# The softmax sums' inverses of an attention phase, sent by the sync engine's queue instead of ScalarE's

## The chip, the cores and the metric

The program runs on one core of one Trainium2 chip. The metric is the device time of one execution in microseconds (us), which is the time of that core. The unchanged kernel took 2614.75 us, the median of 3 runs (2609.27 to 2626.25).

## What is computed

A block of three parts over x of shape 16 x 512 x 256 in fp32: half of a feed-forward part, a causal attention, half of the feed-forward part again. The change lies in the attention:

```python
def _L0_attn_ref(x, Wq, bq, Wkv, bkv, Wo, bo):
    H, DQK, DV = (16, 64, 64)
    b, s, e = x.shape
    q = x @ Wq + bq
    kv = x @ Wkv + bkv
    k, v = jnp.split(kv, [H * DQK], axis=-1)
    q = _rope(q.reshape(b, s, H, DQK).transpose(0, 2, 1, 3))
    k = _rope(k.reshape(b, s, H, DQK).transpose(0, 2, 1, 3))
    v = v.reshape(b, s, H, DV).transpose(0, 2, 1, 3)
    scores = jnp.einsum('bhqd,bhkd->bhqk', q, k) * (1.0 / np.sqrt(DQK))
    scores = jnp.where(causal[None, None], scores, -jnp.inf)
    probs = jax.nn.softmax(scores, axis=-1)
    out = jnp.einsum('bhqk,bhkd->bhqd', probs, v)
    return out.transpose(0, 2, 1, 3).reshape(b, s, H * DV) @ Wo + bo

x = x + 0.5 * _L0_ffn_ref(_layernorm(x), ...)
x = x + _L0_attn_ref(_layernorm(x), ...)
x = x + 0.5 * _L0_ffn_ref(_layernorm(x), ...)
```

## The kernel before, in words

The attention phase works on 16 batches, one after the other, and on the 16 heads of a batch in 8 pairs. So it has 128 units (batch, pair). The order on each engine is written out by hand: `program` calls a function `slot` once per step, and in one slot an engine does the parts of several units that are a few steps apart. `Slot.p` is the number of the pair (0 to 7) within the batch, and `t.has(p + 2)` says that a unit so far ahead or behind exists. The waits are semaphore counts; `need_held` waits and then counts on a semaphore of its own.

What one unit goes through, with the names in the profile:

- TensorE projects queries and keys into `att_ps_z` (L1353), two slots ahead. ScalarE moves them to `att_z_sb` with the bias (L1608).
- The rotary turn needs halves of 32 partitions swapped. SP's queue does it with four DMAs, `swap` (L1370, `att_zs<-att_z_sb`, 128 KB each). GpSimd then multiplies and adds (L1426, L1427, L1429), ScalarE takes the high part of the keys and queries (L1614), GpSimd (L1434) and VectorE (L1500) the low parts.
- TensorE makes the scores (L1765). VectorE adds the mask (L1518) and takes the largest value of each row (L1522). ScalarE takes the exponentials with the sums (L1630): for the four tiles of 128 queries in the order 3, 2, 1, 0. Tiles 3 and 2 go to `att_far`, tiles 1 and 0 to `att_prob`.
- The exponentials of tiles 3 and 2 are turned by way of DRAM: `put` on ScalarE's queue writes `att_far` to `last_tiles_blocks` (L1642, one DMA of 896 KB), `get` on SP's queue reads it in another order into `att_got` in the next slot (L1385, four DMAs of 224 KB), and VectorE transposes blocks of 32 x 32 (`turn`, L1534). `att_got` is a single buffer, so a `get` waits for the `turn` before it.
- The exponentials of tiles 1 and 0 are transposed on TensorE (L1803) and copied by ScalarE in two parts, `copy_near` (L1654) and `copy_next` (L1659).
- TensorE mixes the values (L1818, L1823) into `att_ps_p`.
- The inverse of the sums must stand on all the partitions of a head. VectorE makes it and transposes it (`reciprocals`, L1526 and L1529, into `att_rsumT`). `rows` writes it to DRAM (`inverse_sums`, one DMA of 16 KB). `spread` on SP's queue reads it back, repeated over 64 partitions, into `att_R` (L1377, two DMAs of 128 KB). VectorE multiplies the mixed values by it (`divide`, L1540).
- ScalarE and VectorE split the result into a high and a low part (L1664, L1545), TensorE multiplies by Wo (L1353), and VectorE adds it up in `att_acc` (L1494).
- ScalarE copies the next pair's values to `att_v_sb` (`values`, L1648). TensorE's next projection waits for that copy, because both use the same PSUM bank.

The queue of SP does in one slot, in this order: `swap` of the unit two ahead (it waits for both L1608), `get` of the unit before (it waits for its `put` and for the `turn` before it), `spread` of the same unit (it waits until `rows` has landed), and in three of eight slots a load or store of 512 KB: the residual input at p = 7 (L1402), the next input at p = 0 (L1407), the store of the result at p = 3 (L1413).

`rows` stands on ScalarE's queue before the change: after `copy_next` and before the exponentials of tile 2. `att_rsumT` is a single buffer too: VectorE's next transpose into it waits until `rows` has landed.

## Time and profile before

| | |
|---|---|
| median of 3 runs | 2614.75 us |
| lowest, highest | 2609.27, 2626.25 us |
| the profiled execution | 2626.25 us, of it 2623.5 us from the first to the last instruction |
| TensorE, VectorE, ScalarE, GpSimd busy | 87%, 70%, 55%, 55% of the span |
| granted TensorE clock, mean | 0.974 |
| DMA | 561.57 MB, mean 214 GB/s |

A page of the profile lists per engine the busy time, the groups of instructions by line with the idle time before them and what ended it, and the DMA queues. In the names, PE is TensorE, PEld its weight loads, DVE VectorE, ACT ScalarE, POOL GpSimd, SP SyncE; a "q" behind the name is that engine's sequencer, which issues DMAs and waits while the engine itself may still be busy.

### The profile page before, as it was taken

The numbers are of one execution on the slowest core, as the hardware profiler recorded it, in microseconds if no ns is written. First come the engines' busy times: TensorE is split into PE (matmuls) and PEld (weight loads), VectorE is DVE, ScalarE is ACT, GpSimd is POOL, SyncE is SP. The second block draws the span as 40 slices with busy tenths as digits, with TensorE's granted clock in tenths as the row PEclk, the third lists the DMA queues.
The fourth block names the chain that finished last, engine by engine and source line by source line (L and its number), as shares of the span: only waits on it lengthen the run. The fifth ranks groups of instructions, "written<-read, shape, count | busy, mean of one in ns | idle before, by whom it ended". The sixth has DMA issues, their size and how long they took to land. (4 is left out here: it accounts for less than half of the span.)

```text
span 2623.5 us, 55026 instructions
## 1 busy us (share of the span) xinstructions
PE 2293.0 (87%) x17624; PEld 1793.8 (68%) x17624; DVE 1825.7 (70%) x3128; ACT 1447.8 (55%) x3741; POOL 1434.8 (55%) x1268
## 2 busy tenths in 40 slices
PE   7987899788988988998889889889898878986998
PEld 5753677577777777777777777777777765753676
DVE  5741578487777778777777778778778775741476
ACT  2321444466766766776667667666676652321343
POOL 1100444677677777776677777767777741100342
PEclk9999999899999999999999999999999998999999
DMA  7369553578878888888788887887878876369543
GB/s 249 130 258 409 198 174 119 151 206 220 212 203 222 232 223 220 222 226 215 196 226 219 217 219 214 233 218 205 235 206 223 218 210 214 132 256 409 164 155 101
DMA packets 340248, 561.57 MB, mean 214 GB/s; under 512 B 63616, under 2 KB 274176, under 8 KB 338944
## 3 DMA queue, kind: packets, MB, share of 16 engines
q1 hardware_dynamic: 303104, 438.58, 60.5%
q10 hardware_dynamic: 36864, 119.55, 12.3%
q8 instruction: 139, 2.28, 0.4%
q14 instruction: 141, 1.16, 0.2%
HBM read 329.42 MB, written 161.48 MB: 187 GB/s over the span
## 5 line engine op out<-in xcount | busy, mean ns | idle before, releaser
L1426 POOL TENSOR_TENSOR att_z_sb<-att_z_sb,att_cos 128x512 f32<-128x512 f32 x255 | 336.2, 1318 | 387.9 <-DMA att_zs<-att_z_sb 387.8
L1534 DVE STREAM_TRANSPOSE att_farT<-att_got 128x1792 f32<-128x1792 f32 x128 | 261.0, 2039 | 199.4 <-DMA att_got<-last_tiles_blocks 199.0
L1429 POOL TENSOR_TENSOR att_z_sb<-att_z_sb,att_zs 128x512 f32<-128x512 f32 x255 | 339.3, 1331 | 20.0
L1427 POOL TENSOR_TENSOR att_zs<-att_zs,att_sin 128x512 f32<-128x512 f32 x255 | 342.9, 1345 | 0.0
L1823 PE MATMUL att_ps_p<-att_farT,att_v_sb 128*64 128x128 f32 x3584 | 227.8, 280 | 0.0
L1630 ACT ACTIVATE att_far<-att_ps_w,att_nmax 128x512 f32<-128x512 f32 x256 | 174.2, 688 | 78.2 <-DVE att_nmax L1522 68.6
L1823 PEld LDWEIGHTS att_ps_p<-att_farT,att_v_sb 128*64 128x64 f32 x3584 | 210.7, 142 | 0.0
L1353 PE MATMUL att_ps_z<-att_xT_hi,att_wq_hi 128*128 128x512 f32 x256 | 93.7, 447 | 128.5 <-ACT att_v_sb L1648 123.7
L1434 POOL TENSOR_TENSOR att_kT_lo<-att_z_sb,att_kT_hi 128x512 fp32r<-128x512 f32 x128 | 163.6, 1278 | 47.6 <-ACT att_kT_hi L1614 47.6
L1630 ACT ACTIVATE att_far<-att_ps_x,att_nmax 128x384 f32<-128x384 f32 x256 | 146.6, 578 | 41.6 <-issue 30.0
L1522 DVE TENSOR_REDUCE att_nmax<-att_ps_x 128x2 f32<-128x768 f32 (+1 forms) x256 | 164.9, 686 | 4.4
L1055 POOL TENSOR_TENSOR com_b_kblk<-sh_blkmask,sh_kT 128x128 f32<-128x128 f32 x64 | 32.3, 526 | 242.5 <-POOLq L500 195.0
L1522 DVE TENSOR_REDUCE att_nmax<-att_ps_w 128x2 f32<-128x1024 f32 x128 | 156.7, 1224 | 4.4
L180 POOL TENSOR_SCALAR dis_b_veps<-dis_b_mv 128x4 f32<-128x4 f32 x31 | 13.4, 432 | 266.4 <-DVE dis_b_mv L174 266.4
L1803 PE MATMUL att_ps_z<-sh_ident,att_prob 128*128 128x128 f32 x768 | 140.3, 292 | 3.3 <-ACT att_prob L1630 2.6
L457 ACT ACTIVATE dis_b_prob<-dis_ps_s,dis_b_ebias 128x512 f32<-128x512 f32 x64 | 44.6, 697 | 177.8 <-DVE dis_b_ebias L317 177.8
L1353 PEld LDWEIGHTS att_ps_z<-att_xT_hi,att_wq_hi 128*128 128x128 f32 x256 | 39.1, 192 | 151.5 <-ACT att_v_sb L1648 142.7
L1500 DVE TENSOR_TENSOR att_qT_lo<-att_z_sb,att_qT_hi 128x512 fp32r<-128x512 f32 x128 | 137.0, 1070 | 2.0 <-ACT att_qT_hi L1614 2.0
L1765 PE MATMUL att_ps_x<-att_kT_hi,att_qT_hi 64*128 64x256 f32 (+1 forms) x512 | 128.3, 334 | 4.4 <-ACT att_prob L1630 3.5
L1664 ACT CAST att_oT_hi<-att_ps_p 128x512 fp32r<-128x512 f32 x128 | 75.0, 586 | 99.3 <-DMA att_got<-last_tiles_blocks 69.0
L1608 ACT ACTIVATE att_z_sb<-att_ps_z,att_bk 128x512 f32<-128x512 f32 x128 | 88.5, 691 | 69.9 <-PE att_ps_z L1353 69.9
L1141 PEld LDWEIGHTS com_ps_o<-com_b_U,com_b_pT 128*128 128x128 f32 x512 | 97.9, 192 | 42.6 <-issue 27.7
(248 smaller groups left out, 7171.4 us busy)
## 6 DMA issues: line engine op xcount, KB each, us to landing
last_tiles_blocks<-att_far ACTq DMA_DIRECT2D x128, 896.0 KB, 5.3
att_got<-last_tiles_blocks SPq DMA_DIRECT2D x512, 224.0 KB, 4.8
att_zs<-att_z_sb SPq DMA_DIRECT2D x512, 128.0 KB, 3.2
att_R<-inverse_sums SPq DMA_DIRECT2D x256, 128.0 KB, 3.9
ffn_w<-in_e_W SPq DMA_DIRECT2D x30, 1024.0 KB, 9.4
ffn_wg<-in_e_Wg SPq DMA_DIRECT2D x24, 1024.0 KB, 12.8
x_normalised_transposed<-dis_b_xnT SPq DMA_DIRECT2D x32, 512.0 KB, 3.0
ffn_w<-in_e_W SPq DMA_DIRECT2D x32, 512.0 KB, 15.6
```

The costliest lines, as they stand in the source:

```text
L1353: last = nc.tensor.matmul(ps, lhs[a][ch], rhs[b][ch], start=(i == 0), stop=(i == len(terms) - 1))
L1426: nc.gpsimd.tensor_tensor(z[:, m, i, :], z[:, m, i, :], cos[:], ALU.mult)
L1427: nc.gpsimd.tensor_tensor(zs[:, m, i, :], zs[:, m, i, :], sin[:], ALU.mult).then_inc(sin_s[i].sem, 1)
L1429: nc.gpsimd.tensor_tensor(z[:, m, i, :], z[:, m, i, :], zs[:, m, i, :], ALU.add).then_inc(sum_s[i].sem, 1)
L1434: nc.gpsimd.tensor_tensor(lo[:, u % 2, :], z[:, u % 2, 1, :], hi[:, u % 2, :].bitcast(F32), ALU.subtract)\
L1500: nc.vector.tensor_tensor(lo[:, u % 2, :], z[:, u % 2, 0, :], hi[:, u % 2, :].bitcast(F32), ALU.subtract)\
L1522: nc.vector.tensor_reduce(nmax[:, p % 2, qt, :], scores_of(qt), AX.X, ALU.max, negate=True).then_inc(max_s.sem, 1)
L1534: nc.vector.transpose(farT[:].rearrange("p a (t r) -> p t a r", r=QUAD), got[:]).then_inc(turn_s.sem, 1)
L1630: nc.scalar.activation(dst, src, ACT.Exp, bias=nmax[:, p % 2, qt, hh:hh + 1], accum_out=sums[:, p % 2, hh, qt:qt + 1]).then_inc(exp_s.sem, 1)
L1765: return nc.tensor.matmul(ps, q[a][of_head(hh), p % 2, qt * P:(qt + 1) * P], k[b][of_head(hh), p % 2, 0:wide], start=(m == 0), stop=(m == 2))
L1803: last = nc.tensor.transpose(ps_z[1][:, at:at + P], prob[:, p % 2, hh, PLACE[qt]][:, kb * P:(kb + 1) * P], g.ident[:])
L1823: last = nc.tensor.matmul(mix_bank[of_head(hh), qt * P:(qt + 1) * P], values_of(kb, hh), farT[:, hh * NF + at + kb, :], start=(kb == 0), s ...
```

## The change

`rows` moves from ScalarE's queue to SP's. There it stands between `get` and `spread` of the same unit, with the same two waits: for the transposed inverses, and for the landing of the `spread` before it. Nothing else changes.

```diff
@@ block.sync
+            def rows(j, u):
+                need_held(sp, inv_s, j, 2 * u + 2)
+                need_held(sp, spread_s, j, 32 * u)
+                sp.dma_start(r_dram[u % 2], rsumT[:]).then_inc(row_s.sem, 16)
+
...
                 if t.has(p - 1):
                     get(j, p - 1)
+                    rows(j, p - 1)
                     spread(j, p - 1)
@@ block.scalar
-            def rows(j, u):
-                need_held(act, inv_s, j, 2 * u + 2)
-                need_held(act, spread_s, j, 32 * u)
-                act.dma_start(r_dram[u % 2], rsumT[:]).then_inc(row_s.sem, 16)
-
...
                 if t.has(p - 1):
                     copy_next(j, p - 1)
-                    rows(j, p - 1)
                 if t.has(p):
                     exps(j, p, 2)
                     put(j, p)
```

On ScalarE, in the last slots before the loop over batches, the rows from the second copy to the values' copy stand like this before (L59, L1273 and L1622 belong to waits):

```order
L1614 CAST att_qT_hi<-att_z_sb 128x512
L1273 REGISTER_ALU
L1658 REGISTER_ALU
L1659 COPY att_probT<-att_ps_z 128x256
L59 ISA
L1637 DMA inverse_sums<-att_rsumT 128x32
L1622 REGISTER_ALU
L1630 ACTIVATE att_far,att_sums<-att_ps_x,att_nmax 128x3x4x32 x2
```

and now:

```order
L1620 CAST att_qT_hi<-att_z_sb 128x512
L1273 REGISTER_ALU
L1659 REGISTER_ALU
L1660 COPY att_probT<-att_ps_z 128x256
L1628 REGISTER_ALU
L1636 ACTIVATE att_far,att_sums<-att_ps_x,att_nmax 128x3x4x32 x2
```

The DMA and its held waits are gone between the copy and the exponentials of tile 2; the lines below the change have moved by a few numbers.

On SP's queue, two slots of the same part of the program stand like this before:

```order
L1370 DMA att_zs<-att_z_sb 32x1024 x4
L1385 DMA att_got<-last_tiles_blocks 32x4x448 x4
L1377 DMA att_R<-inverse_sums 64x4x128 x2
L1370 DMA att_zs<-att_z_sb 32x1024 x4
L1385 DMA att_got<-last_tiles_blocks 32x4x448 x4
L1377 DMA att_R<-inverse_sums 64x4x128 x2
```

and now:

```order
L1370 DMA att_zs<-att_z_sb 32x1024 x4
L1390 DMA att_got<-last_tiles_blocks 32x4x448 x4
L1375 DMA inverse_sums<-att_rsumT 128x32
L1382 DMA att_R<-inverse_sums 64x4x128 x2
L1370 DMA att_zs<-att_z_sb 32x1024 x4
L1390 DMA att_got<-last_tiles_blocks 32x4x448 x4
L1375 DMA inverse_sums<-att_rsumT 128x32
L1382 DMA att_R<-inverse_sums 64x4x128 x2
```

The 16 KB write now stands behind all four reads of `get` and directly ahead of the `spread` that waits for it.

## Rows read from the trace of the kernel before

**Rows 1.** Attention phase: us, busy PE, PEld, DVE, ACT, POOL, clock, DMA share, GB/s.

```profile
489.00:2167.00 1678.00, 1467.17 (x13040) 1223.59 (x13039) 1295.05 (x1959) 1143.25 (x3155) 1211.72 (x980) 0.98 0.81 217
```

**Rows 2.** Waits in the same window: us in total, times, longest.

```profile
DVE att_farT L1534 <- DMA att_got<-last_tiles_blocks: 199.0, 76, 7.4
...
PE att_ps_z L1353 <- ACT att_v_sb L1648: 118.4, 94, 3.6
```

**Rows 3.** PE's timeline in a slot without a load: second transposes, next projection.

```profile
1489.17 0.44 PE L1803 MATMUL att_ps_z<-sh_ident,att_prob 128*128 128x128 f32 x2
...
1493.42 0.73 PE L1353 MATMUL att_ps_z<-att_xT_hi,att_wq_hi 128*128 128x512 f32 x2 [1.02 <-ACT att_v_sb L1648]
```

**Rows 4.** ACT's timeline in the same slot.

```profile
1489.64 0.37 ACT L1659 COPY att_probT<-att_ps_z 128x256 f32<-128x256 f32 x1 [0.26 <-PE att_ps_z L1803]
1489.86 0.33 ACTq L1637 DMA_DIRECT2D inverse_sums<-att_rsumT  x1
1490.37 0.58 ACT L1630 ACTIVATE att_far<-att_ps_x,att_nmax 128x384 f32<-128x384 f32 x1 [0.35 <-issue]
...
1492.29 0.59 ACT L1664 CAST att_oT_hi<-att_ps_p 128x512 fp32r<-128x512 f32 x1 [0.68 <-DMA att_got<-last_tiles_blocks]
1492.77 0.59 ACT L1648 COPY att_v_sb<-att_ps_z 128x512 f32<-128x512 f32 x1
```

**Rows 5.** DVE's timeline, same slot: the maxima of tiles 2 and 0, and the turn.

```profile
1488.26 1.29 DVE L1522 TENSOR_REDUCE att_nmax<-att_ps_x 128x2 f32<-128x768 f32 x2
...
1494.59 2.03 DVE L1534 STREAM_TRANSPOSE att_farT<-att_got 128x1792 f32<-128x1792 f32 x1
```

**Rows 6.** Groups by line in the attention phase: tile 2's exponentials, idle time before them.

```profile
L1630 ACT ACTIVATE att_far<-att_ps_x,att_nmax 128x384 f32<-128x384 f32 x256 | 146.6, 578 | 41.6 <-issue 30.0 <-DMA att_R<-inverse_sums 6.2 <-DVE att_nmax L1522 2.8
```

**Rows 7.** ACT's timeline in a slot whose issue waited for the last spread.

```profile
1447.73 0.58 ACT L1630 ACTIVATE att_far<-att_ps_x,att_nmax 128x384 f32<-128x384 f32 x1 [1.55 <-DMA att_R<-inverse_sums]
```

**Rows 8.** What SP's queue waited for in the attention phase: us, times, longest.

```profile
SPq L60 <- DMA inverse_sums<-att_rsumT: 588.2, 126, 8.8
SPq L60 <- ACT att_z_sb L1608: 130.0, 109, 6.5
```

**Rows 9.** SP's queue over the slot of rows 3 to 5.

```profile
1487.95 1.89 SPq L1385 DMA_DIRECT2D att_got<-last_tiles_blocks  x4
1494.74 1.39 SPq L1377 DMA_DIRECT2D att_R<-inverse_sums  x2
1497.26 3.52 SPq L1370 DMA_DIRECT2D att_zs<-att_z_sb  x4
```

**Rows 10.** SP's queue behind the load of the next input (L1407).

```profile
1554.68 1.93 SPq L1385 DMA_DIRECT2D att_got<-last_tiles_blocks  x4
1559.08 1.31 SPq L1377 DMA_DIRECT2D att_R<-inverse_sums  x2
1561.81 3.31 SPq L1370 DMA_DIRECT2D att_zs<-att_z_sb  x4
1566.15 1.93 SPq L1385 DMA_DIRECT2D att_got<-last_tiles_blocks  x4
1572.60 1.59 SPq L1377 DMA_DIRECT2D att_R<-inverse_sums  x2
```

**Rows 11.** ACT's queue in the slot of rows 10.

```profile
1554.26 0.33 ACTq L1637 DMA_DIRECT2D inverse_sums<-att_rsumT  x1
```

**Rows 12.** DVE's turns in the slot of rows 10 and in the next.

```profile
1562.69 2.04 DVE L1534 STREAM_TRANSPOSE att_farT<-att_got 128x1792 f32<-128x1792 f32 x1 [3.62 <-DMA att_got<-last_tiles_blocks]
...
1573.87 2.02 DVE L1534 STREAM_TRANSPOSE att_farT<-att_got 128x1792 f32<-128x1792 f32 x1
```

**Rows 13.** POOL, the turn of the keys that the swap at 1561.81 feeds.

```profile
1569.03 1.30 POOL L1426 TENSOR_TENSOR att_z_sb<-att_z_sb,att_cos 128x512 f32<-128x512 f32 x1
```

**Rows 14.** DMA issues of the page: KB each, median us from issue to landing.

```profile
att_zs<-att_z_sb SPq DMA_DIRECT2D x512, 128.0 KB, 3.2
```

**Rows 15.** A stretch of 6 us behind a load, with the clock (columns as in rows 1).

```profile
1450.00:1456.00 6.00, 5.29 (x22) 3.92 (x24) 1.51 (x4) 3.62 (x12) 2.15 (x2) 0.72 0.95 263
```

## The prediction

> **What bounds the kernel now.** I first took the attention phase as a whole, because the change is nowhere else. It is 1678 us for 128 units, 13.1 us a slot, and no engine fills it: TensorE 1467 us, VectorE 1295, GpSimd 1212, ScalarE 1143, the DMA engines at 0.81 [rows 1]. So the length of a slot is set by chains of waits between engines, and I read the waits next. Two of them matter here: VectorE waits 199.0 us for `att_got` (76 of 128 turns), and TensorE waits 118.4 us for ScalarE's copy of the values (94 slots) [rows 2]. They belong to two kinds of slots.
>
> In a slot without a load or store of 512 KB a loop through TensorE and ScalarE sets the pace. TensorE ends its second transposes about 1489.6 [rows 3]. ScalarE then does `copy_next` (1489.64), the exponentials of tile 2 (from 1490.37), `put`, the high part and the values' copy, which ends at 1492.77 + 0.59 = 1493.36 [rows 4]. TensorE starts the next projection at 1493.42, after 1.02 us of idle time that ended with that copy [rows 3]. VectorE is not in this loop: its maxima for tile 2 end at 1488.26 + 1.29 = 1489.55 [rows 5], and the turn at 1494.59 began without a wait [rows 5].
>
> In the slots around a load or store the transfers set the pace. VectorE stood idle 3.62 us for `att_got` before the turn at 1562.69 [rows 12], and the maxima and the exponentials of the next unit come behind that turn.
>
> The third view is SP's own queue. It waited 588.2 us for `inverse_sums` to land (126 times, 4.7 each) and 130.0 us for `att_z_sb` (109 times, 1.2 each) [rows 8]. The second number is SP's reserve: when `swap` has to wait for ScalarE, SP is early. It has some 1.2 us to give a slot, and in the slots that don't show that wait it has none.
>
> **What goes from ScalarE.** In the slot of [rows 4] `copy_next` ends at 1490.01 and the exponentials begin at 1490.37; the 0.35 us between are put down to issue, that is to the queue that still handles two held waits and the DMA (issued 1489.86, 0.33) while the engine has finished. Over the phase the group shows 41.6 us of idle time: 30.0 of issue, 6.2 of waiting for the `spread` before, 2.8 for the maxima [rows 6]. The waits' view counts the 30.0 over 87 slots with 0.35 each. With the DMA gone the next limit is the maxima, 0.46 us before the copy's end [rows 4, 5], so these 0.35 us go wholly. They lie on the loop of the first kind of slot. Term one: 87 x 0.35 = -30 us.
>
> The 6.2 us fall in slots like the one of [rows 7], where ScalarE stood 1.55 us because the last `spread` had not landed. Such a `spread` is late because the transfers are, and there `att_got` sets the pace. I count nothing for it; its bounds are 0 and -6.2. Back to back instructions on ScalarE overlap by about 0.11 us (the values' copy starts 0.48 us after a cast of 0.59) [rows 4], so the ceiling of the whole saving is 41.6 + 87 x 0.11, about -50 us.
>
> **What comes to SP, in a slot without a load.** The DMA and its two held waits cost SP about what they cost ScalarE, 0.35 us and some 0.1 more; they would come while SP waits for the landing anyway. What counts is when the 16 KB land. In [rows 9] `get` has issued its last read at 1487.95 + 1.89 = 1489.84, and ScalarE issued `rows` at 1489.86 [rows 4]. So on SP it goes out at the same moment, at most 0.2 later. The landing released `spread` at 1494.74, 4.9 us later, and `att_got` had landed by 1494.59 [rows 5]: the 16 KB came home together with the 896 KB ahead of them, so nothing is lost by standing behind them. `spread` ends at 1496.13, the next `swap` begins at 1497.26 [rows 9]. The reserve is 1.1 us; the faster loop takes 0.35 of it and the later landing 0.2 to 0.5. Cover is left; if it is gone, the slot gets no shorter, and the 0.35 are lost.
>
> The Trainium skill ("DMA: Bandwidth & Descriptors", section "Issuing engines are not separate DMA queues") says that issuing from several engines saves only the time on the sequencer. By that the move takes 0.33 us a slot from one sequencer and gives it to another, and changes no transfer. Its section "Queues, rings and completion order" says more: the DMA engines alternate between the queues packet by packet. By that rule the 16 KB on ScalarE's queue pass between the reads of `get` before the change, and can't afterwards, and every slot would lose the lead. Here the trace does not agree for the ordinary slot: there was no lead to lose.
>
> **What comes to SP, behind a load.** Here the order does change. At 1554.26 ScalarE issued `rows` before SP's first read of `get` (1554.68) [rows 10, 11]. It landed by 1559.08, when `spread` began, while `att_got` landed only at 1562.69 [rows 10, 12]. Behind all four reads it lands no earlier than 1562.7. Then `spread` runs 1562.8 to 1564.1 and the next `swap` starts about 1564.3 instead of 1561.81: 2.5 us later. Two things follow.
> - The next `get` starts about 1564.3 + 3.3 + 0.1 = 1567.7 instead of 1566.15 (1.6 later). Its data had landed by 1572.60, and the turn began at 1573.87 without a wait [rows 10, 12]: 1.3 us of cover, so the turn comes 0.3 later.
> - GpSimd's turn of the keys of that `swap` began at 1569.03 [rows 13], back to back. The last of four issues is near 1564.5, and a landing takes 3.2 [rows 14]: 1567.7, so 1.3 us of cover, and GpSimd comes 1.2 later. Whether ScalarE (high part of the keys) then waits can't be read from here; GpSimd has 3.6 us idle a slot [rows 1].
>
> So a batch gives back between 0 and 2.5 us there. I take 1.2, the row nearest to the path: 16 x 1.2 = +19. For the store at p = 3 and the load at p = 7 I take 0.2 each, +6, with 0 and 1.2 as ends. The give-back is 0 to +60 us in all, and 25 is what I take.
>
> **The sum.** -30 + 19 + 6 = -5 us. The profiled execution took 2626.25 us (span 2623.5 and 2.7 around it), so 2621 for its like. That execution is the slowest of the three; on the median of 2614.75 the same change gives 2610 us.
>
> **Rivals.**
> 1. *ScalarE's gap is all that counts.* For it: TensorE's 94 waits for the values' copy. Then -30 - 6 = -36 us, 2579. Against it: 1.9 us a batch is saved in five or six of eight slots, and the slots behind the load are paced by transfers whose amount doesn't change, so that waiting there may simply grow.
> 2. *Slower: SP turns late behind the load.* The mechanism is the lost lead of 3.6 us at one place, the slot after the next input's load. It decides when more than about 1.9 us of the 2.5 reach the path, which is what the batch saves. At the full 2.5 us the cost is +40. A longer stall of TensorE also pulls its clock down: in 1450 to 1456, behind such a load, the granted clock was 0.72 [rows 15], so 6 x 0.28 / 0.5 = 3.4 us at the low level of 1.2 GHz, worth up to 1.7 us of work; in half of the batches +13. Together -30 + 40 + 6 + 13, about +29: 2644. If the lateness is not caught up within the batch, it is more.
> 3. *Nothing moves.* SP's reserve is too small in all slots and its round (swap, get, landing, spread) becomes the loop. Then every gain is eaten: 2615. The waits in [rows 8] speak against it, with 109 waits for `att_z_sb`.
> 4. *Alternating queues,* the rule above, as a mechanism of this kernel: `rows` loses its place between the reads of `get` in the slots where it was issued with or before them. It would cost most where rival 2 looks, and is priced with it. It would be seen as a landing of `inverse_sums` that lags `att_got` in all slots.
>
> **Chances.** Forecast (about -20 to +5 us) 0.45; rival 1 0.20; rival 2 with 4 0.22; rival 3 0.13. A measurement of this kernel tells about 1% (26 us) from no change. Rival 1 ends beyond -1% in most of its cases, 0.18 with the forecast's tail. Rival 2 ends beyond +1% in most of its own, 0.20. The rest is 0.62. The range that leaves two in ten out reaches from most of rival 1 to rival 2's value: 2582 to 2646.
>
> **What would show it.** In the changed profile the idle time before tile 2's exponentials should fall from 41.6 to under 10 us, and the issue part vanish; if not, term one is wrong. SP's wait for `inverse_sums` should stay near 4.5 us in ordinary slots. Behind the load, `spread` should start just behind the landing of `att_got` and the `swap` after it 2 to 3 us later within its slot. VectorE's wait for `att_got` (199 us) should grow by 10 to 40 us: that is where the gain goes. If it stays at 199 and the time falls by 30, rival 1 is right. If GpSimd's wait for `att_zs` or ScalarE's wait for the keys' sum grows and the mean clock falls below 0.97, rival 2 is right.

## The result and the profile after

| | before | after |
|---|---|---|
| median, lowest to highest | 2616.68 us (2609.27 to 2626.25, 4 runs) | 2723.57 us (2718.56 to 2731.76, 4 runs) |
| ratio | | 1.0409, 95% interval 1.0364 to 1.0455 |
| span of the profiled execution | 2623.5 us | 2719.7 us |
| granted TensorE clock, mean | 0.974 | 0.955 |

The change costs 107 us, 4.1%. The forecast was 2610 with a range of 2582 to 2646.

The attention phase, cut so that as much of the program (457 us) lies behind it as in [rows 1], with the same columns:

```profile
489.00:2263.00 1774.00, 1511.63 (x13036) 1262.27 (x13038) 1273.67 (x1956) 1137.48 (x3151) 1200.05 (x978) 0.95 0.75 205
```

It is 96 us longer, which is the whole difference of the spans. TensorE has 13036 matmuls against 13040, yet is busy for 44 us more, at a mean clock of 0.95 instead of 0.98. The other 52 us are idle time of TensorE. Beside the rows on SP's queue nothing was given more to do, and the DMA share fell from 0.81 to 0.75. So the time is waiting, and a lower clock beside it.

First the group of [rows 6], and three of the groups that wait most, in the views by line and by wait (us in total, times, longest):

```profile
L1636 ACT ACTIVATE att_far<-att_ps_x,att_nmax 128x384 f32<-128x384 f32 x256 | 147.2, 583 | 7.2 <-DVE att_nmax L1528 1.9
```

```profile
POOL att_z_sb L1432 <- DMA att_zs<-att_z_sb: 501.9, 126, 9.4
DVE att_farT L1540 <- DMA att_got<-last_tiles_blocks: 331.9, 101, 8.2
...
PE att_ps_p L1818 <- issue: 109.5, 38, 5.1
```

ScalarE's gap is gone as forecast, 41.6 to 7.2 us. But VectorE waits 331.9 us for `att_got` (199.0 before, [rows 2]), and GpSimd waits 501.9 for the `swap` (353.3 before). `get` and `swap` have one thing in common: SP's queue issues both. TensorE's stand before the first mixing matmul (33.8 before) comes behind the late turn. ScalarE has not become free by the lost gap either: it waits earlier in its program, ahead of tile 3's exponentials, for VectorE's maxima, which come behind the turn. The group of before, then the same group now:

```profile
L1630 ACT ACTIVATE att_far<-att_ps_w,att_nmax 128x512 f32<-128x512 f32 x256 | 174.2, 688 | 78.2 <-DVE att_nmax L1522 68.6 <-DVE att_rsum L1526 9.4
```

```profile
L1636 ACT ACTIVATE att_far<-att_ps_w,att_nmax 128x512 f32<-128x512 f32 x256 | 174.0, 686 | 174.1 <-DVE att_nmax L1528 155.0 <-DVE att_rsum L1532 18.8
```

What SP waited for, as in [rows 8]:

```profile
SPq L60 <- DMA inverse_sums<-att_rsumT: 693.6, 128, 9.9
SPq L60 <- ACT att_z_sb L1614: 48.7, 30, 10.8
```

SP now waits for the landing of the rows in every slot. It was held by ScalarE 30 times, where [rows 8] have 109. `swap` waits twice in a slot, for the queries and for the keys: counted by slots, ScalarE held SP in 17 of 128 now and in 73 before. In the other slots `swap` starts late because of SP itself. The next view shows it: SP's queue over two slots without a load, then ScalarE's `put` in them, where [rows 9] has an ordinary slot of before:

```profile
1622.74 2.47 SPq L1370 DMA_DIRECT2D att_zs<-att_z_sb  x4
1625.47 1.83 SPq L1390 DMA_DIRECT2D att_got<-last_tiles_blocks  x4
1627.64 0.34 SPq L1375 DMA_DIRECT2D inverse_sums<-att_rsumT  x1
1634.56 1.30 SPq L1382 DMA_DIRECT2D att_R<-inverse_sums  x2
1636.49 2.61 SPq L1370 DMA_DIRECT2D att_zs<-att_z_sb  x4
1639.43 1.75 SPq L1390 DMA_DIRECT2D att_got<-last_tiles_blocks  x4
1641.51 0.34 SPq L1375 DMA_DIRECT2D inverse_sums<-att_rsumT  x1
1647.47 1.30 SPq L1382 DMA_DIRECT2D att_R<-inverse_sums  x2
```

```profile
1627.53 0.34 ACTq L1643 DMA_DIRECT2D last_tiles_blocks<-att_far  x1
1640.38 0.33 ACTq L1643 DMA_DIRECT2D last_tiles_blocks<-att_far  x1
```

From the start of `swap` to the end of `spread` SP did one thing behind the other: 1622.74 to 1635.86, 13.1 us, and the next `swap` follows 0.6 later. I call it SP's round. The rows went out at 1627.64, just behind the `put` of the next unit (1627.53), and took 6.8 us to land. [Rows 4 and 9] had them out with the end of `get`, two microseconds ahead of the `put`, and home after 4.9.

Worked out from the traces over units 8 to 118: the median round grew from 11.3 to 12.75 us. Up to the end of `get` its median parts did not change (medians 2.5 us for `swap`, 0.3 to the first read, 1.9 for `get`, in both). From there to the start of `spread` it grew from 4.9 to 6.25. The ordinary slot of before is 12.3 to 12.6 us. The rows stand behind the next `put` in none of the 111 slots before and in 48 of them after; those rows land in a mean of 6.8 us, the others in 5.2.

### The profile page after: what moved, and what is told of

It reads as the page before. It is cut to its first block and busy times, and to the rows that moved or that the text cites. A ratio compares the mean times of both kernels' runs of the same rounds, so it can differ in the third digit from the quotient of the medians.

```text
span 2719.7 us, 55138 instructions
## 1 busy us (share of the span) xinstructions
PE 2336.1 (86%) x17624; PEld 1830.2 (67%) x17624; DVE 1806.4 (66%) x3128; ACT 1443.4 (53%) x3741; POOL 1425.0 (52%) x1268
## 5 line engine op out<-in xcount | busy, mean ns | idle before, releaser
L1540 DVE STREAM_TRANSPOSE att_farT<-att_got 128x1792 f32<-128x1792 f32 x128 | 261.5, 2043 | 332.4 <-DMA att_got<-last_tiles_blocks 331.9
L1435 POOL TENSOR_TENSOR att_z_sb<-att_z_sb,att_zs 128x512 f32<-128x512 f32 x255 | 331.1, 1298 | 20.0
L1636 ACT ACTIVATE att_far<-att_ps_w,att_nmax 128x512 f32<-128x512 f32 x256 | 174.0, 686 | 174.1 <-DVE att_nmax L1528 155.0
L1823 PE MATMUL att_ps_p<-att_farT,att_v_sb 128*64 128x128 f32 x3584 | 257.3, 302 | 0.0
L1823 PEld LDWEIGHTS att_ps_p<-att_farT,att_v_sb 128*64 128x64 f32 x3584 | 239.2, 156 | 0.0
L180 POOL TENSOR_SCALAR dis_b_veps<-dis_b_mv 128x4 f32<-128x4 f32 x31 | 13.4, 431 | 264.4 <-DVE dis_b_mv L174 264.4
L1818 PE MATMUL att_ps_p<-sh_kT,att_v_sb 128*64 128x256 f32 x256 | 48.9, 462 | 97.9 <-issue 81.5
L1818 PE MATMUL att_ps_p<-att_probT,att_v_sb 128*64 128x128 f32 (+1 forms) x768 | 90.5, 343 | 45.1 <-issue 28.0
L394 PE MATMUL dis_ps_s<-dis_b_xnT,sh_G 128*128 128x512 f32 x256 | 120.6, 615 | 6.3 <-ACT dis_b_xnT L452 4.6
## 6 DMA issues: line engine op xcount, KB each, us to landing
ffn_wg<-in_e_Wg SPq DMA_DIRECT2D x24, 1024.0 KB, 13.1
```

Source lines behind the costliest of these rows:

```text
L1435: nc.gpsimd.tensor_tensor(z[:, m, i, :], z[:, m, i, :], zs[:, m, i, :], ALU.add).then_inc(sum_s[i].sem, 1)
L1540: nc.vector.transpose(farT[:].rearrange("p a (t r) -> p t a r", r=QUAD), got[:]).then_inc(turn_s.sem, 1)
L1636: nc.scalar.activation(dst, src, ACT.Exp, bias=nmax[:, p % 2, qt, hh:hh + 1], accum_out=sums[:, p % 2, hh, qt:qt + 1]).then_inc(exp_s.sem, 1)
L1818: nc.tensor.matmul(mix_bank[of_head(hh), kb * P:NEAR * P], values_of(kb, hh), src[:, at:at + WIDTH[kb]], start=(kb == 0), stop=(kb == NEAR ...
L1823: last = nc.tensor.matmul(mix_bank[of_head(hh), qt * P:(qt + 1) * P], values_of(kb, hh), farT[:, hh * NF + at + kb, :], start=(kb == 0), s ...
```

## The experiments

Each run stood beside runs of the kernel before on the same chip (2611 to 2624 us). Diffs are against the kernel before, or against the changed kernel where this is said.

**1. The rows ahead of `get` on SP's queue** (against the changed kernel).

```diff
+                    rows(j, p - 1)
                     get(j, p - 1)
-                    rows(j, p - 1)
```

> The changed kernel with one line moved: on SP's queue rows stands ahead of get instead of behind it. Theory A (serial round): SP's queue does swap, get, rows, the landing of rows and spread one behind the other, 2.7 + 2.1 + 6.2 + 1.5 us = 12.5 us with nothing beside it, and a late slot cannot be caught up, since a late get now makes a late rows. Then rows ahead of get starts the landing 2 us earlier, and get is issued beside it: the time falls back to that of the kernel before or below it, 2580 to 2625 us, and SP again waits for att_z_sb in some 100 slots. Theory B (SP's queue simply has too much to issue: one more DMA and two more held waits, about 0.45 us a slot): those are still there, so it stays near 2700 us. Theory C (lost stall cover: the earlier exponentials on ScalarE make put collide with get): also stays near 2700.

Measured: 2561.94 us, ratio 0.9767 [0.9732, 0.9802]. The same queue with the same number of issues is 162 us faster, so neither SP's issue time nor its queue is by itself the cost. What differs is when the rows land. The pages' rows of DMA issues (KB each, median us from issue to landing), of before, of after and of this run:

```profile
inverse_sums<-att_rsumT ACTq DMA_DIRECT2D x128, 16.0 KB, 4.7
```

```profile
inverse_sums<-att_rsumT SPq DMA_DIRECT2D x128, 16.0 KB, 5.7
```

```profile
inverse_sums<-att_rsumT SPq DMA_DIRECT2D x128, 16.0 KB, 1.8
```

**2. The rows on ScalarE's queue, behind `put`.**

```diff
-                    rows(j, p - 1)
                 if t.has(p):
                     exps(j, p, 2)
                     put(j, p)
+                if t.has(p - 1):
+                    rows(j, p - 1)
```

> The kernel before with rows left on ScalarE's queue, but behind put instead of ahead of the exponentials of tile 2, so about 2 us later and behind the 896 KB of put. SP's queue issues nothing more than in the kernel before. Theory A (what counts is when the 16 KB land, because SP's queue stands still until then): as slow as the changed kernel or slower, 2700 to 2780 us. Theory B (too much to issue on SP) and theory D (the 16 KB are slow because they are in SP's ring instead of ScalarE's): within 1% of the kernel before, 2600 to 2640 us.

Measured: 2809.45 us, 1.0702 [1.0669, 1.0736]. Late rows cost on ScalarE's queue too, and more: behind the `put` in all 111 slots, 5.9 us to land.

**3. No rows at all.** The inverse sums never go to DRAM; `spread` reads data that were put there once, and waits only for the `spread` before. VectorE's wait for the landing of the rows is left out too.

```diff
-                need_held(sp, row_s, j, 16 * (u + 1))
+                need_held(sp, spread_s, j, 32 * u)
...
...
-                    rows(j, p - 1)
```

> The kernel before without rows: the inverses of the sums are never written to DRAM in the loop (inverse_sums is filled once with other data), and spread does not wait for them, but only for the spread before it; so the division uses wrong numbers. It leaves out 128 DMAs of 16 KB and SP's wait for their landing. Theory A: this wait (588 us over 126 slots in the kernel before) is part of what sets the slots behind a load, and ScalarE's 0.35 us of issue sets the others: 2540 to 2600 us. If SP's wait did not matter in the kernel before, only the 30 us of ScalarE come off: 2580 to 2590 us.

Measured: 2507.71 us, 0.9545 [0.9513, 0.9577]. The rows cost 117 us in the kernel before, more than either expectation had (it is 32 us under the lower end).

**4. `get` ahead of `swap` on SP's queue.**

```diff
+                if t.has(p - 1):
+                    get(j, p - 1)
                 if t.has(p + 2):
                     swap(j, p + 2)
                 if t.has(p - 1):
-                    get(j, p - 1)
                     spread(j, p - 1)
```

> The kernel before, with get ahead of swap on SP's queue; rows stays on ScalarE, in its old place. get can then start when put has landed, some 1 to 4 us earlier, and rows comes well behind it, as in the changed kernel relative to get, but without SP being in its way. Theory A (what counts is how long SP's queue stands between its last issue and the landing of rows): swap now fills part of that stand, so SP's round gets no longer, 2560 to 2620 us. If instead the position of the 16 KB behind the 896 KB is bad by itself, whatever SP does meanwhile: slower, 2640 to 2700 us. A cost of its own: swap comes later for GpSimd.

Measured: 2655.47 us, 1.0123 [1.0095, 1.0152]. The first theory's 2560 to 2620 missed; the time lies where the second had it. Its reason, the place behind the 896 KB, does not fit: the rows landed in 4.1 us, sooner than before. What the trace shows is the cost that was named last, the late `swap` (GpSimd waits 458 us for it, 353 before).

**5. The rows on GpSimd's queue**, between its rotation of the queries and the keys' low part.

```diff
@@ block.gpsimd
                         rotate(j, p + 1, 0)
+                if t.has(p - 1):
+                    rows(j, p - 1)
+                if t.has(p + 1):
                     key_low(j, p + 1)
```

> rows on GpSimd's queue, between the rotation of the queries and the low part of the keys; ScalarE's queue is freed as in the changed kernel, SP's queue is as in the kernel before. Theory A: the issue does not depend on SP's own progress any more, so no serial round; the time is near the kernel before, 2590 to 2640 us, less ScalarE's 0.35 us a slot if GpSimd issues in time, more if GpSimd is late (it finishes the rotation of the queries about 1 us behind the time at which ScalarE issued rows) or pays over 1 us for the issue. Theory B (freed ScalarE is what made it slow, by an earlier put): about 2700.

Measured: 2574.64 us, 0.9823 [0.9776, 0.987]. ScalarE is freed here as in the changed kernel, and in runs 1 and 10 too, and all three are fast: an earlier `put` alone does not make the kernel slow.

**6 and 7. The two input loads of a batch cut to 64 B per partition**, once in the changed kernel and once in the kernel before. The residual and the later batches' inputs are not loaded whole.

```diff
-                        sp.dma_start(xres[:], tiles(x_dram, j + 1)).then_inc(xres_in.sem, 16)
+                        sp.dma_start(xres[:, 0, 0:16], tiles(x_dram, j + 1)[:, 0, 0:16]).then_inc(xres_in.sem, 16)
...
+                        sp.dma_start(xin[:, 0, 0:16], tiles(x_dram, j + 1)[:, 0, 0:16]).then_inc(x_in.sem, 16)
```

> The changed kernel with the two loads of 512 KB per batch (residual input at p = 7, next input at p = 0) cut to 64 bytes a partition; so the rest of their tiles is old data. To be compared with e7, the kernel before with the same cut. Theory A': the lateness begins behind the loads and is then carried on by SP's serial round. Then without them the round (12.5 us less what the emptier DMA engines give) fits into a slot of 12.3 us, and the changed kernel is at most 10 us slower than e7, or up to 30 us faster. If the round is too long by itself, loads or not, e6 stays 60 us or more above e7.

> The kernel before with the same two loads cut to 64 bytes a partition (the rest of their tiles is old data). Its slots 0 and 1 of each batch (13.4 and 15.6 us against 12.4 for the ordinary ones) should lose most of their excess: 16 x 3 to 4 us, so 2560 to 2590 us.

Measured: 2659.96 us after, 2553.75 before. Both gain 64 to 67 us, and the difference stays: 106 us. The slowdown does not need the loads, so rival 2's place is not its cause.

**8. The rows on ScalarE's queue, one place earlier**, behind tile 3's exponentials and ahead of the high part of the queries.

```diff
                 if t.has(p):
                     exps(j, p, 3)
+                if t.has(p - 1):
+                    rows(j, p - 1)
...
-                    rows(j, p - 1)
```

> rows on ScalarE's queue, but earlier: behind the exponentials of tile 3, ahead of the high part of the queries, so about 1.5 us earlier than in the kernel before and mostly ahead of get's reads. ScalarE still pays for the issue. Theory A: the time follows the landing of the 16 KB; e2 moved the issue 2 us later and took 190 us more; this one moves it ahead of get, as e1 did (which took 160 us off the changed kernel and left 2.3 us instead of 5 for the landing): 2555 to 2600 us. Rival (what helped in e1 was ScalarE's freed queue, 0.35 us a slot): then this one stays within 1% of the kernel before, 2600 to 2640 us.

Measured: 2528.03 us (2521.37 to 2535.15), 0.9654 [0.9623, 0.9685]. This version computes all and beats both kernels: by 3.5% the one before, by 7.2% the changed one. It is 27 us under the range that was expected. What SP waited for:

```profile
SPq L60 <- ACT att_z_sb L1608: 380.7, 216, 12.3
SPq L60 <- DMA inverse_sums<-att_rsumT: 242.8, 92, 7.5
```

SP is early again: ScalarE holds it in 115 of 128 slots, and it waits 242.8 us for the rows instead of 588.2. Its median round is 8.4 us.

**9. Rows that nobody reads.** ScalarE issues them where it did, into another tensor; `spread` is as in the run without rows.

```diff
-                act.dma_start(r_dram[u % 2], rsumT[:]).then_inc(row_s.sem, 16)
+                act.dma_start(junk[u % 2], rsumT[:]).then_inc(row_s.sem, 16)
```

> The kernel before, with ScalarE issuing the rows where it did, but into a tensor that nobody reads; the spread waits for the previous spread alone (it leaves out the inverse sums of the rows, so the output differs). It splits the 117 us by which the kernel without rows beat before. If ScalarE's issue ahead of its tile-2 exponentials is worth what the prediction's first term says (30 us), this run is 30 us slower than the kernel without rows: 2538, and the idle time ahead of the tile-2 exponentials is 30 to 45 us, as in before. If that issue lies beside other work, it stays within 10 us of the kernel without rows: 2508 to 2518, with the same 30 to 45 us idle. If the rows cost through the load that they put on the DMA queues and not through SP's wait for them, it is near before: 2600 or more.

Measured: 2550.08 us, 0.9729 [0.9708, 0.975]. The 117 us split into 42 for ScalarE's issue and its bytes (2550 - 2508) and 73 for SP's wait (2623 - 2550, against the runs of before on this chip; run 3 stood on another). The group ahead of tile 2's exponentials, of this run and of the run without rows:

```profile
L1638 ACT ACTIVATE att_far<-att_ps_x,att_nmax 128x384 f32<-128x384 f32 x256 | 146.7, 578 | 40.2 <-issue 37.3 <-DVE att_nmax L1530 1.5
```

```profile
L1633 ACT ACTIVATE att_far<-att_ps_x,att_nmax 128x384 f32<-128x384 f32 x256 | 147.2, 586 | 0.6
```

**10. The rows amid the reads**, after two of the four (against the changed kernel).

```diff
                 for kb in range(QB):
+                    if kb == QB // 2:
+                        rows(j, u)
                     sp.dma_start(got[kb * QUAD:(kb + 1) * QUAD]...
...
-                    rows(j, p - 1)
```

> The changed kernel with the rows issued after two of the four reads of the last tiles instead of behind all four. Theory that the length of SP's round decides (rows land later, so the spread, so the next swap): the row is issued 1.0 us earlier than in the changed kernel and 1.1 later than in the kernel with the rows ahead of the reads, so the time lies between 2562 and 2724, 2600 to 2680, and SP's wait for inverse_sums between 3 and 9.9 us per wait. Theory that the row is slow only because it stands behind the whole 224 KB on the same queue, each read of it alike: the same middle, as two of four are 112 KB. Theory that what matters is whether the row is out before ScalarE's put: a threshold, either under 2590 or over 2700.

Measured: 2557.21 us, 0.9764 [0.9741, 0.9788], below the range that I gave to the first two theories. (The expectation's 224 and 112 KB should read 896 and 448: each of the four reads has 224 KB.) The edit moves the rows ahead of two reads and wins 166 us. They land in 3.7 us instead of 5.7, the round is 9.9 us, and SP is early again, with the rows ahead of every `put`:

```profile
SPq L60 <- DMA inverse_sums<-att_rsumT: 351.7, 128, 6.1
SPq L60 <- ACT att_z_sb L1615: 205.4, 158, 11.5
```

So the cost looks like a threshold and not like a slope: 1.9 us of landing time between this run and run 1 cost nothing, and the next 2.0 cost 166 us. Which threshold was still open: the `put`, or the slot's length.

**11. The rows on GpSimd's queue, held until SP has issued `get`** (against run 5).

```diff
+                need_held(pool, read_s, j, u + 1)
                 pool.dma_start(r_dram[u % 2], rsumT[:]).then_inc(row_s.sem, 16)
```

> The kernel with the rows on GpSimd's queue (2575), with GpSimd made to wait until SP has issued the four reads of the same unit; SP's queue holds no more than there, and the row is not behind the reads on its own queue. If what costs is that the row waits for SP's progress (a late SP makes a late row, the row then stands behind ScalarE's put, and SP is later still), it is well above 2575, towards the changed kernel: 2640 to 2740, with SP's wait for inverse_sums above 9 us. If what costs is SP's own issue time or the place behind the reads on SP's queue, it stays within 1% of 2575 (2560 to 2600). GpSimd's own wait for SP can add a part; it shows as idle time ahead of key_low's subtraction.

Measured: 2754.14 us, 1.0494 [1.0456, 1.0532], 180 us above run 5. The time fits the first theory, SP's wait does not: 731.9 us over 128 times, 5.7 each and not above 9. The rows were ahead of the `put` in 79 of 111 slots and behind it in 32, so the `put` can't be ruled out here. GpSimd's own wait clouds the size, since what it does next is late too:

```profile
L1443 POOL DMA_DIRECT2D inverse_sums<-att_rsumT x128 | 75.1, 587 | 487.3 <-SPq L1394 458.4 <-DMA att_R<-inverse_sums 23.5 <-issue 5.5
```

**12. The four `swap` copies on GpSimd's queue**, between its rotations (against the changed kernel).

```diff
+                if t.has(p + 2):
+                    swap(j, p + 2)      # block.gpsimd, behind rotate(j, p + 1, 1)
```

> The changed kernel (rows behind the reads on SP) with the four swap copies issued by GpSimd between its two rotations instead of by SP: SP's round is shorter by the 2.7 us that the swap takes and by its wait for the raw queries and keys. If the length of SP's round of about 12.8 us against a slot of 12.3 is what costs the 107 us, it falls back to 2560 to 2630, with SP waiting for att_z_sb nowhere, for att_rsumT or last_tiles_blocks instead, and rows mostly ahead of the put. If what costs is only that the row stands behind the reads and lands late, it stays at 2690 to 2730. GpSimd's own load (four more issues per slot, in front of the queries' rotation) could keep it from the full gain.

Measured: 2868.0 us, 1.0958 [1.0924, 1.0993]. The expectation missed. GpSimd spent 246.6 us on the issues and 265.4 us waiting for ScalarE ahead of them, and ScalarE then waited 336.9 us for GpSimd's queries. The edit put new waits on GpSimd and ScalarE, and the run tells nothing about SP's round.

**13 and 14. One `swap` copy of 128 partitions instead of four of 32**, in the changed kernel and in the kernel before. Same bytes; the exchange of the blocks is left out.

```diff
-                for at in range(0, P, 32):
-                    sp.dma_start(zs[at:at + 32, u % 2], z[at ^ 32:(at ^ 32) + 32, u % 2]).then_inc(swap_s[u % 2].sem, 16)
+                sp.sem_inc(swap_s[u % 2].sem, 48)
+                sp.dma_start(zs[:, u % 2], z[:, u % 2]).then_inc(swap_s[u % 2].sem, 16)
```

> The changed kernel with the swap issued as one copy of 128 partitions instead of four of 32: the same bytes, three issues fewer on SP (about 2 us of its round), no load added elsewhere; the rows stay behind the reads. It leaves out the exchange of the 32-partition blocks, so the output differs. Theory that SP's round, longer than a slot, is the cause: the round falls from 12.8 to about 10.8 us, below the slot's 12.3, and the time falls to 2550 to 2600, with rows ahead of the put again. Theory that the place of the row behind the reads (late landing, late spread) is the cost by itself: 2690 to 2730, since nothing moves between reads and row.

> The kernel before with the swap as one copy (leaves out the exchange of the blocks, so the output differs). Theory of SP's round: 11.3 falls to about 9.3 us, no slot is over 12.3 any more, and the 73 us by which the kernel whose rows nobody reads beats before should mostly go: 2550 to 2575. If the changed kernel with one swap lands within 20 us of this one, the change's whole cost is the round. Theory that the row's landing is a cost by itself: 2610 to 2625, as before.

Measured: 2569.58 us (0.9823 [0.9757, 0.9888]) and 2565.81 us (0.9811 [0.9749, 0.9873]). `swap` takes SP 0.5 us instead of 2.5. The two orders then differ by 4 us (each ratio is known to about 0.7%, 17 us), where they differed by 107. In the changed kernel with one copy the rows still stand behind all four reads and land as late as before this edit, and SP waits for them longer:

```profile
inverse_sums<-att_rsumT SPq DMA_DIRECT2D x128, 16.0 KB, 5.6
```

```profile
SPq L60 <- DMA inverse_sums<-att_rsumT: 726.9, 128, 10.3
SPq L60 <- ACT att_z_sb L1614: 90.8, 67, 11.6
```

So most of the 107 us need a round without room. What the place behind the reads costs by itself is not told apart here: in the kernel before with one copy the rows also go out behind all four reads (a median of 1.25 us behind), and the changed kernel spares ScalarE its issue (a gap of 2.6 us against 39.2), which can hide a cost of up to the 42 us of run 9. The edit also brings `get` forward, so these two runs alone do not tell a shorter round from earlier reads. And a longer wait (726.9 against 693.6) goes with 154 us less time: the sum of a wait does not say what it costs.

**15. Eight `swap` copies of 16 partitions** in the kernel before.

```diff
-                for at in range(0, P, 32):
+                for at in range(0, P, 16):
```

> The kernel before with the swap issued as eight copies of 16 partitions instead of four of 32: the same bytes, four more issues on SP (about 2.7 us of its round); the rows stay on ScalarE in their place, and the reads stand against them as before or later. Theory of SP's round: 11.3 + 2.7 = 14.0 us, over a slot, so it is as slow as the changed kernel or slower: 2700 to 2860, with SP waiting for inverse_sums over 100 times and for att_z_sb hardly. Theory that the row's place behind the reads on SP's queue is the cost: this run keeps the rows ahead, so 2610 to 2650.

Measured: 2766.01 us, 1.0566 [1.0489, 1.0642]. The time is as expected, the waits are not: SP waited 192 times for `att_z_sb` (228.2 us) and 63 times for the rows. The median round did not grow to 14.0 either: it is 11.4 us, since the rows, issued beside a later `get`, land in 2.2 us. So this kernel is slow with a round as before. The longer `swap` (5.1 us) makes itself and `get` late in slots where SP was early: GpSimd waits 457.5 us for `att_zs` and VectorE 328.3 us for `att_got`. The run does not show the round alone; the next two do.

**16 and 17. Six `spread` copies instead of two**, same bytes, behind everything else of SP's round; in the kernel before, and in the fast version of run 8.

```diff
-                for hh in range(2):
+                for hh, b, n_b in [(0, i, 1) for i in range(4)] + [(1, 0, 2), (1, 2, 2)]:
```

> The kernel before with the spread issued as six copies instead of two (one half block by block, the other in two pieces; the same bytes), so that SP's round gets some 2.6 us longer behind the reads and behind the landing of the rows, while nothing ahead of them changes. Theory of SP's round: 11.3 + 2.6 = 13.9 us is over the slot of 12.3, so lateness is carried into the next swap and reads: 2680 to 2780, and SP's wait for att_z_sb falls from 109 times to under 50. Theory that only a late get or a late row within the slot costs: both stand where they stood, so 2610 to 2640.

> The same six copies in the kernel with the rows early on ScalarE's queue (2528), where SP's round is 8.4 us. Theory of SP's round: 8.4 + 2.6 = 11.0 us stays under the slot, so hardly anything is lost: 2525 to 2555, though before loses 70 to 160 us by the same edit. Theory that more issues or more, smaller copies cost by themselves, whatever the round: it loses as much as before does by the same edit.

Measured: 2724.62 us (1.0389 [1.0361, 1.0418]) in the kernel before, 2595.47 (0.9912 [0.988, 0.9944]) in the fast version. The first is as slow as the changed kernel, with the rows in their old place and ahead of every `put`. Its SP waits look like those of the changed kernel in one sign, 41 waits for ScalarE (in 24 slots) instead of 109 (in 73):

```profile
SPq L60 <- DMA inverse_sums<-att_rsumT: 403.6, 94, 7.1
SPq L60 <- ACT att_z_sb L1608: 57.5, 41, 9.9
```

The control lost 67 us where I expected at most 27. Its median round went from 8.4 to 11.2, under the slot. But by the mean length of each of the eight slots of a batch, nearly all of the loss is in the two around the load of the next input: 13.6 and 14.4 us instead of 12.2 and 12.6. There SP issues one DMA more and transfers land later. The other six changed by 0 to 0.4 each, 16 us over the 16 batches. In the kernel before the same edit costs 89 of 108 us in those six slots and 19 around the load. This is what sets the two apart: in the ordinary slots the longer round costs where it passes the slot, and hardly where it does not.

The kernels in which SP's order, or the rows' place, is the main thing that differs (round and landing worked out from the traces, units 8 to 118):

| kernel | rows land, median us | SP's round, median us | rounds over 12.3 us, of 111 | time, us |
|---|---|---|---|---|
| rows early on ScalarE | 3.4 | 8.4 | 6 | 2528 |
| rows ahead of `get` on SP | 1.8 | 8.6 | 0 | 2562 |
| rows on GpSimd | 4.6 | 9.9 | 15 | 2575 |
| rows amid `get` | 3.7 | 9.9 | 8 | 2557 |
| before, one swap | 4.7 | 10.8 | 24 | 2566 |
| before, small loads | 4.7 | 11.1 | 3 | 2554 |
| after, one swap | 5.6 | 11.2 | 24 | 2570 |
| rows early, six spreads | 3.5 | 11.2 | 27 | 2595 |
| before | 4.7 | 11.3 | 28 | 2617 |
| after, small loads | 5.6 | 12.6 | 65 | 2660 |
| after | 5.7 | 12.75 | 68 | 2724 |
| before, six spreads | 4.1 | 13.5 | 70 | 2725 |
| rows behind `put` | 5.9 | 13.5 | 97 | 2809 |

Up to a round of 11.2 the time lies within some 70 us. Beyond it the time rises steeply, in this table whatever made the round long. The median is not the whole law: the last two rows have the same round and differ by 85 us, and the count of rounds over a slot's 12.3 us follows the time more closely. Nor is the round the only way to be slow. Four runs are left out because the edit changed something else that engines wait for: run 4 (another order of `swap` and `get`, 2655 us), run 11 (12.35 us, GpSimd held, 2754), run 12 (no `swap` in the round, 2868), and run 15, whose 2766 us stand beside a round of 11.4.

## Why the prediction was wrong

- **What bounds the kernel now.** Half right. The loop through TensorE and ScalarE is there, and it is what run 9 against the run without rows prices. The third view was read wrongly. "It has some 1.2 us to give a slot" is a mean over the waits for `att_z_sb`, taken as a reserve of the whole queue. `swap` waits twice in a slot, so the 109 waits lie in 73 of 128 slots; in the other 55 ScalarE did not hold SP. And 28 of 111 rounds of before were already over 12.3 us: those had nothing to give. "VectorE is not in this loop" holds for the slot of [rows 3 to 5]; in the changed kernel its maxima, behind the late turn, are what ScalarE waits for (174.1 us, 78.2 before).
- **Term one (-30 us).** Right in mechanism and place: the gap fell from 41.6 to 7.2 us. Its worth, by run 9 against the run without rows, is about 42 us, bytes included, between the 30 and the ceiling of 50. It does not show in the result because ScalarE now waits longer earlier in its slot, ahead of tile 3's exponentials.
- **The 6.2 us counted as nothing.** Not told apart by any run.
- **SP's issue cost, "they would come while SP waits for the landing anyway".** Half right. The DMA's own 0.34 us lie within the landing, which starts with the issue. What stands ahead of it does not: the rows go out a median of 0.33 us behind the end of `get` where they went out 0.14 ahead of it, 0.5 us later and not "at most 0.2".
- **"Nothing is lost by standing behind them."** This is the step that failed. I read from one slot [rows 5, 9] that the 16 KB came home with the reads anyway. In the median slot that was so (0.1 us behind the last read). But in 42 of 111 slots of before they landed more than 0.5 us ahead of it, 0.8 us ahead by the mean of all; in the changed kernel in none, 0.4 us behind by the mean. Over all slots they took 5.7 us instead of 4.7, and 3.7 or 1.8 where they stand behind two reads or none. With the 0.5 above, that is the 1.5 us by which the round grew (11.3 to 12.75), beyond "0.2 to 0.5", and beyond the cover of 1.1. By means, 1.2 of the 1.6 us between `get` and `spread` are this lead, and 0.35 are reads that land later themselves.
- **"If it is gone, the slot gets no shorter."** Wrong in sign. A round longer than a slot hands its lateness to the next `swap` and `get`. On ScalarE the rows went out by ScalarE's time, and a late SP could catch up. On SP they are late when SP is late. Then the `put`, which does not wait for the `get` of that slot, goes out ahead (48 of 111), the landing takes 6.8 us, and SP is later still. Run 16 against its control, run 17, shows that a round longer than the slot is enough for a kernel as slow as the changed one, with the rows ahead of every `put`, and runs 13 and 14 that most of the 107 us go with a shorter one. That the `put` adds to it is read from the landings of the two kinds of slots and was not tried alone.
- **Behind a load, +19 and +6.** Right in kind, far too small, and not the cause of the rest. The rows of a batch's first unit landed a mean of 3.0 us ahead of the reads before and 0.5 behind now, the lost lead that I had read. Of the 99 us that the eight slots of a batch add up to over 16 batches, the two around the load bring 57 and the six others 42. But with the loads cut to 64 B, after stays 106 us above before.
- **The choice among the rivals.** Rival 3 named the mechanism (SP's round becomes the loop) and priced it at nothing lost, 2615. With what the runs measured its price would be: a round of 12.75 and 0.3 to 0.6 to the next `swap` is 13.1 to 13.4 us, over 12.5 us for the slot of run 9, for 128 slots: +77 to +115 us over 2550. That is 2627 to 2665. The rest of the way to 2724 no run takes apart; slots in which the round is far over the median (19 us between the two puts around the load at 1608.32) and TensorE's clock must be in it.
- **The clock.** Rival 2's signs came true, a mean of 0.955 against 0.974 and a longer wait of GpSimd for `att_zs` (501.9 us, 353.3 before), though not by rival 2's cause. VectorE's wait for `att_got` grew by 133 us and not by 10 to 40. 44 of the 96 us are TensorE being busy longer with the same matmuls. I take the clock for a follower, which no run tries alone: TensorE's long stands, such as 4.86 us ahead of the mixing matmul at 1608.41, come behind a turn that waited for its reads.

```profile
1606.27 2.05 DVE L1540 STREAM_TRANSPOSE att_farT<-att_got 128x1792 f32<-128x1792 f32 x1 [7.89 <-DMA att_got<-last_tiles_blocks]
1608.41 1.12 PE L1818 MATMUL att_ps_p<-sh_kT,att_v_sb 128*64 128x256 f32 x4 [4.86 <-issue]
```

- **The rule of alternating queues.** "There was no lead to lose" holds for the median slot and not for the 42 above. What the runs show is that the order of issue counts more than the queue: run 11 issues the rows on another queue a median of 0.6 us behind the reads, and they land in 4.9 us, 0.2 behind the last read; run 1 issues them on the reads' own queue ahead of them, and they land in 1.8. The Trainium skill ("DMA: Bandwidth & Descriptors", "Queues, rings and completion order") has each DMA engine alternate between queues by packet; by that rule the rows of run 11 should have landed ahead of the reads, and in the median slot they did not. The same page of the Trainium skill says that issuing from several engines "will only save the time on the sequencer" ("Issuing engines are not separate DMA queues"). That time was 0.33 us a slot here; but with another queue comes another order of issue, the place behind the reads on SP's queue cost 107 us, and one place earlier on ScalarE's own queue gained 93.

## What to carry to other kernels

When a queue waits for the landing of its own small transfer, add up its whole round (every issue, the landing from the moment of issue, every wait that starts late when the queue is late) and set it against the slot. While it is well shorter in every slot, it cost little here; beyond that, lateness is handed on. Count the slots in which the queue was held by nobody (55 of 128 here) and the rounds that are over a slot already (28 of 111), and not the mean of its waits, for the reserve. A small write that something waits for goes out ahead of large transfers, by the engine that is early; one place earlier in ScalarE's program brought 3.5%, one queue further lost 4.1%.

## What the hardware showed that was not expected

A 16 KB write took a median of 1.8 us to land ahead of 896 KB of reads, 3.7 behind half of them and 5.7 behind all on the same queue; 4.7 to 4.9 about or behind the end of their issue on another queue; and 5.9 behind 896 KB of writes as well, on the writes' queue. And SP's queue can wait more and cost less: 726.9 us of waiting for the rows at 2570 us, 693.6 at 2724.
